# Attention stage: rounded projections with their orders, one instruction over two banks for maxima and exponentials, the last recurrence ahead of V's rows

## The chip, the core and the metric

One NeuronCore of a Trainium2 chip runs the whole program in one launch. The metric is the device time in microseconds; lower is better. The engines are PE (matmuls; PEld is its weight load), DVE (VectorE), ACT (ScalarE), POOL (GpSimd) and SP (queues DMAs). Each works through its own instructions in the order in which they are written and waits on counting semaphores for the others.

## The reference

A token tower over x of 32 sequences of 256 tokens, width D = 192: four recurrent blocks, one attention block of 12 heads of width 16, and one quantised feed-forward block.

```python
def _block(x, g, bt, Wi, bi, cw, cb, wd, bd_, wB, bB_, wC, bC_, wo, bo):
    h = _layernorm(x, g, bt)
    uv = h @ Wi.T + bi
    u, v = (uv[..., :D], uv[..., D:])
    uc = _dwconv_causal(u, cw, cb)
    delta = jax.nn.softplus(uc @ wd.T + bd_)
    Bm = uc @ wB.T + bB_
    Cm = uc @ wC.T + bC_
    y = _selective_scan(uc, delta, Bm, Cm)
    y = y * jax.nn.sigmoid(v)
    return x + (y @ wo.T + bo)
...
x = embedding[tokens] + pos_enc[:S][None]
...
h = h + _L0_attn_ref(_layernorm(h, axis=-1), wq, bq, wk, bk, wv, bv, wo, bo)
h = h + _L0_ffn_ref(_layernorm(h, axis=-1), weight_t, bias)
```

The attention takes q (scaled by 1/4), k and v from three projections of the normalised rows, turns part of q and k by the rope angles, and computes softmax(q k^T) v and an output projection. The normalisation in front of it has no gain or bias.

## The kernel before

**Two stages.** Rows lie in `x` (SBUF) from the first gather to the end. The first stage (`steps`, 67 steps) runs 64 items, 16 for each of the four layers, an item being four tiles of 128 rows (two sequences). The second stage (`steps2`, 37 steps, m = 2 to 38) runs 32 sequences of 256 rows through attention and feed-forward. Both are software pipelines written out by hand: in a step, every engine does a different piece of the work for items of different lags. `at(k)` is the item or sequence k steps behind. Nothing sets the order but the text of each engine's `step` and `step2` and the semaphores.

**Step 2 on PE** has six groups g = 0 to 5. In each: the transposed scores of `at(4)` (`scores_t`, L759, four matmuls over 64 rows, into banks `B_ST`), the plain scores of `at(2)` (`scores`, L746, into `B_S`, for the row maxima), the transposes that turn the heads of `at(2)` (`turn_heads`, L732, `identr,parts`), and something of its own. Group 0 ends with `turn_x1` (L704 and L706, `ident,xn`) and has the last of the value products (`values`, L775, also in groups 2 and 4); group 1 begins with `turn_max` (L787) and ends with `project_qk` for the first 128 rows (L711, L712); group 2 has `turn_back` (L816) and ends with `project_qk` for the other 128 rows; group 3 ends with `project_v` (L718, L721); group 4 has `turn_o` (L704, L706), group 5 begins with `project_o` (L718, L721 with `w_out`) and ends with `feed_forward`.

**The projections** of Q, K and V take full f32 operands: `h1_t`, the turned rows, as the stationary operand, in two parts of 128 and 64 rows of the contraction, and `w_qkv` as the moving one. The program has one matmul for each part; the trace shows each full-f32 matmul as two instructions. Transposes and everything declared `F32R` are one instruction each.

**Their input.** `norm_rows` (DVE, L1395) writes (x - mean) * rstd of two tiles to `xn1`; `turn_x1` turns it into `B_H1`; `save_h1` (ACT, `turned`, L1061 and L1062) copies it to `h1_t`. `inverse_deviation2` (POOL, L466 to L478, seven small instructions) gives `rstd2` for it and for the second normalisation `xn2` of `at(6)`.

**The chains around the scores.** `maxima` (DVE, L1406) reduces each of the two score banks with an instruction of its own. `exps` (ACT, L1071) does the same with exponentials of the two `B_ST` banks. `scores` of a group waits for `maxima` of the group before and for `save_heads` (ACT, L1081 and L1082) of its own; `scores_t` of a group waits for `exps` of the group before. ACT's order in a group is `exps`, `save_heads`, then, in group 0, `save_o` (L1110, L1111) and `save_h1`; `save_max` (L1103) opens group 1; `high_parts` (L1092) ends groups 3 and 4. `save_qk` (DVE, L1416) takes q and k from their banks; POOL's `rotate` turns them, ACT's `high_parts` rounds them, POOL's `low_parts` (the end of `rotate`, L499) takes the remainder; `parts` is what `turn_heads` of the next step turns. `quantise` is DVE's three passes on `xn2` (L1456, L1459, L1464), `finish` its last one (L1473).

**The seam.** In the last step of the first stage, `step` at l = 4, k = 2, the attention of sequence 0 begins. DVE does `save_qk` twice and `save_v`; then, in `step2` at m = 2 (`early`), the `recurrence` of the last item (L1319 to L1341). PE's `rows` of that item (L676 to L686) needs its `hc_l` (L1341).

## Time and profile before

| | us |
|---|---|
| median of 3 runs | 1655.63 (1651.02 to 1657.86) |
| the profiled execution | 1659.81 |
| its span from the first instruction to the last | 1657.9 |
| PE busy in the span | 1555.3 (94%) |
| DVE busy | 1365.5 (82%) |
| ACT busy | 1238.9 (75%) |
| POOL busy | 747.5 (45%) |

The span is what the trace covers; 1.9 us of the profiled execution lie outside it. Busy time counts a matmul from its start to the end of its last write, so PE can show as busy while the next matmul could not yet start; the distance from one start to the next is the measure for what a matmul costs.

### The profile page before, as it was taken

How to read it: one execution, taken by the hardware profiler on the slowest of the kernel's cores; microseconds unless marked ns; L12 is line 12 of the kernel's file. 1: busy time of each engine (PE TensorE's matmuls, PEld its weight loads, DVE VectorE, ACT ScalarE, POOL GpSimd, SP SyncE). 2: the span in 40 equal slices, each digit the busy share in tenths (PEclk: the TensorE clock that was granted, in tenths of full speed). 3: DMA queues.
4: the chain of work that ended last, by engine and by line, in shares of the span. 5: the costliest groups of instructions: out<-in, count | busy, mean ns of one | idle time of the engine just before them, and what ended most of it. 6: DMA issues, size and time to landing. Idle time of an engine off the chain costs nothing.

```text
span 1657.9 us, 36360 instructions
## 1 busy us (share of the span) xinstructions
PE 1555.3 (94%) x11137; PEld 1229.3 (74%) x11137; DVE 1365.5 (82%) x3414; ACT 1238.9 (75%) x2875; POOL 747.5 (45%) x1354
## 2 busy tenths in 40 slices
PE   3699999999999999999999988999999999999985
PEld 2578788878888888888888875666666666666653
DVE  4699999889999899999999875678888878888864
ACT  2587788688888778888888844677777777777763
POOL 6656633223333233333333244555565555555542
PEclk9799999999999999999999995999999999999997
DMA  7121100000000000000000000000000000000000
GB/s 165 31 59 28 23 8 1 1 33 0 0 1 1 1 1 0 0 1 1 1 0 0 1 1 1 2 7 11 11 10 15 10 10 10 10 10 10 15 12 25
DMA packets 16397, 21.98 MB, mean 13 GB/s; under 512 B 2928, under 2 KB 13808, under 8 KB 16304
## 3 DMA queue, kind: packets, MB, share of 16 engines
q1 hardware_dynamic: 13232, 14.54, 2.7%
q0 software_dynamic: 3072, 6.30, 2.4%
q8 instruction: 47, 0.77, 0.2%
q14 instruction: 46, 0.38, 0.1%
HBM read 14.14 MB, written 6.29 MB: 12 GB/s over the span
## 4 chain that ended last, share of the span: by engine, by line
PE 62%; ACT 14%; DVE 12%; issue 9%; POOL 1%; DMA 1%; DVEq 1%; ACTq 0%; POOLq 0%
PE bank L595 9%; PE bank L586 7%; PE bank L775 5%; PE bank L732 4%; PE bank L746 4%; PE bank L718 4%; PE bank L759 4%; PE bank L711 3%; PE bank L721 3%; PE bank L712 3%; PE bank L676 3%; ACT xs L1028 2%; DVE x L1360 2%; ACT ht L1018 2%; PE bank L606 2%
## 5 line engine op out<-in xcount | busy, mean ns | idle before, releaser
L1071 ACT ACTIVATE probs<-bank 128x512 f32<-128x512 f32 x384 | 207.1, 591 | 133.8 <-PE bank L759 131.0
L1406 DVE TENSOR_REDUCE mx<-bank 128x2 f32<-128x512 f32 x384 | 246.1, 682 | 26.6 <-PE bank L746 25.0
L441 POOL TENSOR_TENSOR x<-x,bo_row 128x768 f32<-128x768 f32 (+1 forms) x64 | 118.9, 1858 | 188.0 <-DVE ucr_r L1305 188.0
L586 PE MATMUL bank<-ht,w_uv 128*128 128x512 f32 x576 | 171.0, 407 | 16.5 <-ACT sv_l L1051 11.5
L759 PE MATMUL bank<-q_t,k_t 64*128 64x256 f32 x768 | 157.2, 353 | 8.7 <-ACT probs L1071 5.5
L417 POOL TENSOR_TENSOR lnt<-mv,const 128x4 f32<-128x4 f32 x64 | 20.5, 321 | 311.9 <-DVE mv L1270 311.8
L746 PE MATMUL bank<-k_t,q_t 64*128 64x256 f32 x768 | 141.2, 325 | 6.2 <-ACT k_t L1082 3.1
L1296 DVE SCALAR_TENSOR_TENSOR uc_h<-u_h,vec,uc_h 128x512 f32<-128x512 f32 x192 | 143.9, 750 | 2.9 <-ACT uc_h L989 2.9
L586 PEld LDWEIGHTS bank<-ht,w_uv 128*128 128x128 f32 x576 | 111.2, 196 | 46.3 <-issue 16.6
L1279 DVE SCALAR_TENSOR_TENSOR xs<-x,rstd,xs 128x192 fp32r<-128x192 f32 x256 | 90.0, 413 | 59.4 <-ACT xs L1028 59.4
L759 PEld LDWEIGHTS bank<-q_t,k_t 64*128 64x128 f32 x768 | 103.0, 188 | 39.7 <-issue 21.3
L499 POOL TENSOR_TENSOR parts<-qk_rows,parts 128x192 fp32r<-128x192 f32 x128 | 77.8, 628 | 99.9 <-ACT parts L1092 99.8
L586 PE MATMUL bank<-ht,w_uv_rest 128*128 128x512 f32 x384 | 122.0, 400 | 0.0
L968 ACT ACTIVATE u_l<-bank,vec 64x256 f32<-64x256 f32 x128 | 60.0, 469 | 78.1 <-PE bank L586 77.3
L985 ACT ACTIVATE uc_l<-bank,vec 64x256 f32<-64x256 f32 x128 | 71.9, 561 | 60.9 <-DVE inp_l L1322 59.9
L595 PE MATMUL bank<-ucr_h,w_z 128*128 128x512 f32 x256 | 107.5, 420 | 5.6 <-ACT ht L1018 5.4
L746 PEld LDWEIGHTS bank<-k_t,q_t 64*128 64x128 f32 x768 | 99.1, 194 | 16.0 <-ACT k_t L1082 9.1
L732 PE MATMUL bank<-identr,parts 128*128 128x128 f32 x768 | 105.9, 263 | 2.2 <-issue 2.1
L1081 ACT ACTIVATE q_t<-bank 128x256 fp32r<-128x256 f32 x192 | 73.5, 383 | 45.0 <-PE bank L732 44.9
L775 PE MATMUL bank<-probs,v_aug 128*32 128x256 f32 x1536 | 104.5, 390 | 0.2 <-issue 0.2
L1018 ACT ACTIVATE ht<-bank 128x512 fp32r<-128x512 f32 x192 | 100.8, 598 | 4.8 <-PE bank L647 3.3
L647 PE MATMUL bank<-identr,xs 128*128 128x128 f32 x768 | 76.2, 247 | 29.1 <-DVE xs L1279 18.3
(178 smaller groups left out, 4668.9 us busy)
## 6 DMA issues: line engine op xcount, KB each, us to landing
out_dram<-y_out SPq DMA_DIRECT2D x32, 192.0 KB, 2.0
raw_z<-w_z_dram SPq DMA_DIRECT2D x4, 704.0 KB, 5.3
raw_uv<-w_uv_dram SPq DMA_DIRECT2D x4, 576.0 KB, 3.9
emb<-embedding_dram,idx POOLq DMA_INDIRECT x64, 3.6
q_t<-mx_t SPq DMA_DIRECT2D x64, 6.0 KB
w_o<-w_o_dram SPq DMA_DIRECT2D x1, 768.0 KB, 5.4
bo_row<-bout_dram SPq DMA_DIRECT2D x4, 96.0 KB, 6.6
w_qkv<-w_qkv_dram SPq DMA_DIRECT2D x1, 288.0 KB, 7.1
```

What stands on the lines that cost most here:

```text
L441: nc.gpsimd.tensor_tensor(rows, rows, bo_row[:, l, :][:, None, :].broadcast_to([P, CT, D]), ALU.add).then_inc(x_biased, 1)
L586: last = nc.tensor.matmul(out[:], w, r[:], start=(k == 0), stop=(k == len(passes) - 1))
L595: last = nc.tensor.matmul(out[:], w, r[:, b, :], start=(k == 0), stop=(k == len(passes) - 1))
L732: last = nc.tensor.transpose(B_HEADS[g][:, (2 * o + t) * P:(2 * o + t + 1) * P].bitcast(F32R), parts[:, s, t, o, 2 * g:2 * g + 2, :].rearr ...
L746: last = nc.tensor.matmul(B_S[j][:, t * S:(t + 1) * S], q_t[q, s, g, t * P:(t + 1) * P], k_t[q, s, g, :], start=True, stop=True)
L759: last = nc.tensor.matmul(B_ST[j][:, t * S:(t + 1) * S], k_t[q, s, g, t * P:(t + 1) * P], q_t[q, s, g, :], start=True, stop=True)
L775: last = nc.tensor.matmul(bank[32 * h:32 * h + 32, c:c + S], v_aug[:, s, t, 4 * p + h, :], probs[:, (s + p) % 2, h // 2, (2 * (h % 2) + t) ...
L1018: last = act.activation(ht[g][:], B_T[g][:], ACT.Identity)
L1071: last = act.activation(probs[:, (s + g // 2) % 2, g % 2, 2 * j * S:2 * (j + 1) * S], B_ST[j][:], ACT.Exp, scale=float(DH) ** -0.5)
L1279: last = nc.vector.scalar_tensor_tensor(out=xs[:, k, D:2 * D], in0=x[:, tile_of(c, k)], scalar=rstd[:, s, k:k + 1], in1=xs[:, k, 0:D].bitc ...
L1296: nc.vector.scalar_tensor_tensor(out=uc, in0=uk, scalar=v(l, part, V_W0 + k), in1=uc, op0=ALU.mult, op1=ALU.add).then_inc(taps, 1)
L1406: last = nc.vector.tensor_reduce(mx[:, s, :, j * H // 2 + g], B_S[j][:].rearrange("p (t k) -> p t k", t=2), AX, ALU.max)
```

## The change

- PSUM is declared as four pairs of banks instead of eight banks. The two score banks are neighbours now, and so are the two banks of transposed scores. `maxima` and `exps` become one instruction over both banks.
- The Q, K and V projections take F32R operands in five passes over 128 contraction rows each: the rounded rows and the rest of the rows, packed in three groups of 128, against rounded weights, and two more passes against the rest of the weights. The weights are centred beforehand (their column means subtracted), so that the rows need no mean subtracted.
- `norm_rows` for `xn1` becomes `round_rows2` on POOL (x * rstd, rounded, both tiles in one instruction) and `rest_of_rows2` on DVE (x * rstd less the rounded part). `turn_x1` is six F32R transposes in two halves (four at the end of group 0 into `B_H1`, two in group 1 after `turn_max` into the other half of `B_MT`'s bank); `save_x1` copies them in two instructions, the second at the head of group 1.
- The weights are loaded in layer 0 (SP, after the last gather is placed) and prepared in layer 3: means in steps 3 and 4 (PE), centring in steps 4 and 5 (DVE), rounding in step 14 (ACT), the rest in step 15 (DVE).
- POOL's order in a step is `inverse_deviation2`, `rotate` of the first 128 rows, `round_rows2`, V's rows, `rotate` of the others, `low_parts`. The third pass of `quantise` moves from the end of a step to the next one, behind `norm_variances`. On ACT in group 4, the copies of the turned output (`B_OTT`) go ahead of `exps`.
- At the seam, the last `recurrence` is split and stands between and behind the two `save_qk`, ahead of `save_v`.

```diff
-            return ctx.enter_context(nc.psum_tensor(name, [P, 512], F32))
+            return ctx.enter_context(nc.psum_tensor(name, [P, 2, 512], F32))
...
-        w_qkv = sb("w_qkv", [P, 2, 3 * D])
+        w_qkv = sb("w_qkv", [P, 3, 3 * D], F32R)
+        w_qkv_rest = sb("w_qkv_rest", [P, 2, 3 * D], F32R)
...
-        xn1 = sb("xn1", [P, 2, 2, D])
-        h1_t = sb("h1_t", [P, 2 * S])
+        xs1 = sb("xs1", [P, 2, 2, 2 * D], F32R)
+        h1_t = sb("h1_t", [P, 2, 3, P], F32R)
...
-        (B_UH, B_VH, B_UVL, B_ZH, B_ZCL, B_BH, B_BL, B_CH) = [ps(f"bank{i}") for i in range(8)]
+        banks = [ps(f"banks{i}") for i in range(4)]
+        (B_UH, B_ZH, B_BH, B_BL, B_VH, B_UVL, B_ZCL, B_CH) = [banks[i // 2][:, i % 2, :] for i in range(8)]
...
+        QKV_SPREAD, QKV_MEANS, QKV_CENTRE, QKV_ROUND, QKV_SPLIT = 2, (3, 4), (4, 5), 14, 15
+        QKV_COLS = ((0, 2 * D), (2 * D, 3 * D))
...
+        B_SS, B_SST = banks[1][:], banks[0][:]
...
+                if l == 1:
+                    sp.wait_ge(x_loaded, NCH)
+                    sp.dma_start(raw_qkv, w_qkv_d).then_inc(s_w2, 16)
...
+            def rounded_there(m, it):
+
+                if it is not None:
+                    wait(pool, rstd2_ready, m + 1)
+                    wait(pool, t1_done, 2 * (it[0] - 1))
+
+            def round_rows2(it):
+                if it is None:
+                    return
+                n, s = it
+                nc.gpsimd.tensor_tensor(xs1[:, s, :, 0:D], x[:, bass.ds(n * 2 * D, 2 * D)].rearrange("p (k d) -> p k d", d=D),
+                                        rstd2[:, 0:2][:, :, None].broadcast_to([P, 2, D]), ALU.mult
+                                        ).then_inc(xs1_rounded, 1)
...
+                inverse_deviation2(at(None))
+                rounded_there(at(None), at(0))
+                if at(1) is not None:
+                    rotate(at(1), 0)
+                round_rows2(at(0))
...
-                inverse_deviation2(at(None))
                 it = at(1)
                 if it is not None:
-                    rotate(it)
+                    n, s = it
+                    rotate(it, 1)
+                    for t in range(2):
+
+                        wait(pool, hi_ready, 2 * n + t + 1)
+                        if t == 1 and at(0) is not None:
+
+                            wait(pool, xn1_ready, at(0)[0] + 1)
+                        low_parts(s, t)
...
+            def qkv_mean(part):
+
+                lo, hi = QKV_COLS[part]
+                pe.wait_ge(s_w2, W2_ALL)
+                pe.wait_ge(mean_spread, 1)
+                nc.tensor.matmul(B_VH[:, 0:hi - lo], gain_rows[:, 0, :], raw_qkv[:, 0, lo:hi], start=True, stop=False)
+                nc.tensor.matmul(B_VH[:, 0:hi - lo], gain_rows[0:LO, 1, :], raw_qkv[0:LO, 1, lo:hi], start=False,
+                                 stop=True).then_inc(qkv_means, 1)
...
-                rows_turned(xn1[:, s], B_H1, ident[:]).then_inc(t1_done, 1)
+                for k, (t_, g_) in enumerate(X1_PARTS[4:] if second else X1_PARTS[:4]):
+                    dst = B_H2[:, S + k * P:S + (k + 1) * P] if second else B_H1[:, k * P:(k + 1) * P]
+                    last = nc.tensor.transpose(dst.bitcast(F32R), xs1[:, s, t_, g_ * P:(g_ + 1) * P], identr[:])
+                last.then_inc(t1_done, 1)
+
+            def qkv_product(t_, cols, dst):
+                passes = ((0, w_qkv[:, 0, cols]), (1, w_qkv[:, 1, cols]), (2, w_qkv[:, 2, cols]),
+                          (0, w_qkv_rest[:, 0, cols]), (1, w_qkv_rest[:, 1, cols]))
+                for k, (g_, w) in enumerate(passes):
+                    last = nc.tensor.matmul(dst, h1_t[:, t_, g_, :], w, start=(k == 0), stop=(k == len(passes) - 1))
+                return last
...
-                wait(pe, h1_ready, n + 1)
-                rows_times(h1_t, t, w_qkv, slice(0, 2 * D), B_QK[t][:, 0:2 * D]).then_inc(qk_done, 1)
+                wait(pe, h1_ready, 2 * n + 2)
+                qkv_product(t, slice(0, 2 * D), B_QK[t][:, 0:2 * D]).then_inc(qk_done, 1)
...
-                both_rows_times(h1_t, w_qkv, slice(2 * D, 3 * D), B_V).then_inc(v_done, 1)
+                for t in range(2):
+                    last = qkv_product(t, slice(2 * D, 3 * D), B_V[:, t * D:(t + 1) * D])
+                last.then_inc(v_done, 1)
...
+                if l == L - 1 and k in QKV_CENTRE:
+                    pe.wait_ge(qkv_centred, 3 * (QKV_CENTRE.index(k) + 1))
...
-                for j in range(2):
-                    last = act.activation(probs[:, (s + g // 2) % 2, g % 2, 2 * j * S:2 * (j + 1) * S], B_ST[j][:], ACT.Exp,
-                                          scale=float(DH) ** -0.5)
-                last.then_inc(exp_done, 1)
+                act.activation(probs[:, (s + g // 2) % 2, g % 2, :].rearrange("p (j k) -> p j k", j=2), B_SST, ACT.Exp,
+                               scale=float(DH) ** -0.5).then_inc(exp_done, 1)
...
+                        if at(1) is not None:
+                            save_x1(at(1)[0], True)
                         save_max(at(3))
-                    exps(at(4), g)
                     if g == 4 and at(5) is not None:
                         turned(B_OTT, or_t, ott_done, at(5)[0], ott_saved)
+                    exps(at(4), g)
                     save_heads(at(2), g)
...
+            def centre_qkv(part):
+
+                lo, hi = QKV_COLS[part]
+                dve.wait_ge(qkv_means, part + 1)
+                for p in range(3):
+                    nc.vector.tensor_tensor(raw_qkv[:, p, lo:hi], raw_qkv[:, p, lo:hi], B_VH[:, 0:hi - lo],
+                                            ALU.subtract).then_inc(qkv_centred, 1)
+
+            def split_qkv():
+                dve.wait_ge(qkv_rounded, 3)
+                for p in range(2):
+                    nc.vector.tensor_tensor(w_qkv_rest[:, p, :], raw_qkv[:, p, :], w_qkv[:, p, :].bitcast(F32),
+                                            ALU.subtract).then_inc(qkv_split, 1)
...
+            def rest_of_rows2(m, it):
+                if it is None:
+                    return
+                n, s = it
+                wait(dve, xs1_rounded, n + 1)
+                for k in range(2):
+                    last = nc.vector.scalar_tensor_tensor(out=xs1[:, s, k, D:2 * D], in0=x[:, rows_of(n, k)],
+                                                          scalar=rstd2[:, k:k + 1], in1=xs1[:, s, k, 0:D].bitcast(F32),
+                                                          op0=ALU.mult, op1=ALU.subtract)
+                last.then_inc(xn1_ready, 1)
...
-                for j in range(2):
-                    last = nc.vector.tensor_reduce(mx[:, s, :, j * H // 2 + g], B_S[j][:].rearrange("p (t k) -> p t k", t=2),
-                                                   AX, ALU.max)
-                last.then_inc(max_done, 1)
+                nc.vector.tensor_reduce(mx[:, s].rearrange("p t (j h) -> p j t h", j=2)[:, :, :, g],
+                                        B_SS.rearrange("p j (t k) -> p j t k", t=2), AX, ALU.max).then_inc(max_done, 1)
...
                     save_qk(seq(0), 0)
+                    recurrence_high(item(ITEMS - 1))
                     save_qk(seq(0), 1)
+                    recurrence_rest(item(ITEMS - 1))
                     save_v(seq(0))
...
+                if l == L - 1 and k == QKV_SPREAD:
+                    dve.wait_ge(means_done, L)
+                    nc.vector.memset(gain_rows[:], 1.0 / D).then_inc(mean_spread, 1)
+                if l == L - 1 and k == QKV_SPLIT:
+                    split_qkv()
...
-                    recurrence(item(ITEMS - 1))
...
                     norm_variances(first, second)
+                quantise(at(7), 2)
                 save_qk(at(1), 0)
...
-                if first is not None:
-                    wait(dve, t1_done, first[0] - 1)
-                norm_rows(m, first, 0, xn1[:, at(0)[1]] if first is not None else None, xn1_ready)
+                rest_of_rows2(m, first)
...
-                quantise(second, 2)
```

PE, the last steps written out before the loop of the second stage, from the last values of group 0 to `turn_back` of group 2. Before:

```order
L775 MATMUL bank<-probs,v_aug 32x256 x8
L704 MATMUL bank<-ident,xn 128x128 x2
L706 MATMUL bank<-ident,xn 64x128 x2
L787 MATMUL bank<-ident,mx 12x128 x2
L759 MATMUL bank<-q_t,k_t 128x256 x4
L746 MATMUL bank<-k_t,q_t 128x256 x4
L732 MATMUL bank<-identr,parts 128x128 x4
L711 MATMUL bank<-w_qkv,h_t 128x384
L712 MATMUL bank<-w_qkv,h_t 128x384
L759 MATMUL bank<-q_t,k_t 128x256 x4
L746 MATMUL bank<-k_t,q_t 128x256 x4
L816 MATMUL bank<-ident,o_t 128x128 x3
```

The same place after the change:

```order
L829 MATMUL banks<-probs,v_aug 32x256 x8
L854 MATMUL banks<-identr,xs 128x128 x4
L841 MATMUL banks<-ident,mx 12x128 x2
L854 MATMUL banks<-identr,xs 128x128 x2
L813 MATMUL banks<-q_t,k_t 128x256 x4
L800 MATMUL banks<-k_t,q_t 128x256 x4
L786 MATMUL banks<-identr,parts 128x128 x4
L861 MATMUL banks<-w_qkv,h_t 128x384 x3
L861 MATMUL banks<-w_qkv_rest,h_t 128x384 x2
L813 MATMUL banks<-q_t,k_t 128x256 x4
L800 MATMUL banks<-k_t,q_t 128x256 x4
L885 MATMUL banks<-ident,o_t 128x128 x3
```

Two of the six transposes of the rows now stand behind `turn_max`, and a projection is five matmuls in a row.

DVE, the same steps, from the end of one to the middle of the next. Before:

```order
L1406 TENSOR_REDUCE mx<-bank 128x2 x2
L1464 TENSOR_SCALAR xq<-xn 128x384
L1473 SCALAR_TENSOR_TENSOR y_out<-bank,x 128x384
L1406 TENSOR_REDUCE mx<-bank 128x2 x2
L1379 BN_STATS st<-x 128x6 x4
L1406 TENSOR_REDUCE mx<-bank 128x2 x2
L1386 BN_AGGR mv<-st 128x2 x4
L1416 TENSOR_TENSOR qk_rows<-bank,b_qkv 128x384
```

After the change:

```order
L1521 TENSOR_REDUCE mx<-banks 128x2x2
L1587 SCALAR_TENSOR_TENSOR y_out<-banks,x 128x384
L1521 TENSOR_REDUCE mx<-banks 128x2x2
L1484 BN_STATS st<-x 128x6 x4
L1521 TENSOR_REDUCE mx<-banks 128x2x2
L1491 BN_AGGR mv<-st 128x2 x4
L1578 TENSOR_SCALAR xq<-xn 128x384
L1530 TENSOR_TENSOR qk_rows<-banks,b_qkv 128x384
```

The write of `xq` has moved past `y_out`, two maxima and both statistics instructions.

DVE at the seam, from the last rows of `x` of the second-last item on. Before:

```order
L1416 TENSOR_TENSOR qk_rows<-bank,b_qkv 128x384 x2
L1425 COPY v_rows<-bank 128x384
L1319 SCALAR_TENSOR_TENSOR inp_h<-bank,vec,uc_h 128x512
L1322 SCALAR_TENSOR_TENSOR inp_l<-bank,vec,uc_l 128x256
L1328 SCALAR_TENSOR_TENSOR hs_h<-dc_h,inp_h 128x256 x2
L1332 SCALAR_TENSOR_TENSOR hs_l<-dc_l,inp_l 128x256
L1337 SCALAR_TENSOR_TENSOR hc_h<-bank,vec,hs_h 128x512
L1341 TENSOR_TENSOR hc_l<-cb_l,hs_l 128x256
```

After the change:

```order
L1530 TENSOR_TENSOR qk_rows<-banks,b_qkv 128x384
L1419 SCALAR_TENSOR_TENSOR inp_h<-banks,vec,uc_h 128x512
L1422 SCALAR_TENSOR_TENSOR inp_l<-banks,vec,uc_l 128x256
L1428 SCALAR_TENSOR_TENSOR hs_h<-dc_h,inp_h 128x256 x2
L1530 TENSOR_TENSOR qk_rows<-banks,b_qkv 128x384
L1437 SCALAR_TENSOR_TENSOR hs_l<-dc_l,inp_l 128x256
L1442 SCALAR_TENSOR_TENSOR hc_h<-banks,vec,hs_h 128x512
L1446 TENSOR_TENSOR hc_l<-cb_l,hs_l 128x256
L1539 COPY v_rows<-banks 128x384
```

The recurrence's first half fills the time between the two `save_qk`, and the copy of V's rows comes last.

## Rows read from the trace of the kernel before

**Rows 1.** Windows: engine busy us in each stretch, granted PE clock, DMA share, GB/s.

```profile
1072.50:1552.50 480.00, 472.15 (x4197) 320.50 (x4193) 388.78 (x900) 360.32 (x1023) 278.67 (x550) 1.00 0.03 10
```

**Rows 2.** Timeline, PE, one step: start, length in us, instruction, [idle before].

```profile
1250.97 0.91 PE L711 MATMUL bank<-w_qkv,h_t 128*128 128x384 f32 x2
...
1254.39 0.92 PE L718 MATMUL bank<-w_qkv,h_t 128*128 128x192 f32 x4
...
1256.55 0.44 PE L704 MATMUL bank<-ident,o_rows 128*128 128x128 f32 x2
...
1264.16 0.44 PE L704 MATMUL bank<-ident,xn 128*128 128x128 f32 x2
...
1264.93 0.38 PE L787 MATMUL bank<-ident,mx 128*12 128x128 f32 x2
1265.24 0.50 PE L759 MATMUL bank<-q_t,k_t 64*128 64x256 f32 x4
...
1265.91 0.54 PE L732 MATMUL bank<-identr,parts 128*128 128x128 f32 x4
1266.28 0.88 PE L711 MATMUL bank<-w_qkv,h_t 128*128 128x384 f32 x2
...
1267.53 0.38 PE L746 MATMUL bank<-k_t,q_t 64*128 64x256 f32 x1
...
1268.41 0.55 PE L816 MATMUL bank<-ident,o_t 128*128 128x128 f32 x3
...
1270.21 0.91 PE L711 MATMUL bank<-w_qkv,h_t 128*128 128x384 f32 x2
```

**Rows 3.** Timeline, PE, F32R passes of a recurrent layer, 512 and 256 columns.

```profile
405.29 0.39 PE L595 MATMUL bank<-ucr_h,w_z_rest 128*128 128x512 f32 x1
405.52 0.40 PE L595 MATMUL bank<-ucr_l,w_z_rest 128*128 128x512 f32 x1
...
406.10 0.28 PE L606 MATMUL bank<-ucr_h,w_z_rest 128*128 128x256 f32 x1
406.22 0.28 PE L606 MATMUL bank<-ucr_l,w_z_rest 128*128 128x256 f32 x1
```

**Rows 4.** Lines, PEld over the span: busy us, mean ns, idle before.

```profile
L606 PEld LDWEIGHTS bank<-ucr_r,w_z 128*128 128x128 f32 x128 | 24.4, 191 | 0.0
```

**Rows 5.** Timeline, ACT, groups 0 to 1 of the step of rows 2.

```profile
1265.84 1.05 ACT L1071 ACTIVATE probs<-bank 128x512 f32<-128x512 f32 x2
...
1267.06 0.36 ACT L1082 ACTIVATE k_t<-bank 128x256 fp32r<-128x256 f32 x1
```

**Rows 6.** Timeline, DVE and POOL, end of the step of rows 2.

```profile
1259.11 0.36 DVE L1459 TENSOR_SCALAR xn<-xn 128x384 f32<-128x384 f32 x1
...
1261.90 1.00 POOL L456 TENSOR_TENSOR x<-x,b_ffn 128x384 f32 x1
1262.02 1.10 DVE L1464 TENSOR_SCALAR xq<-xn 128x384 bf16<-128x384 f32 x1
...
1263.51 1.28 DVE L1406 TENSOR_REDUCE mx<-bank 128x2 f32<-128x512 f32 x2
```

**Rows 7.** Timeline, PE, the seam, with its idle time and what ended it.

```profile
987.44 1.05 PE L680 MATMUL bank<-ones,hc_h 128*128 128x1 f32 x8 [3.60 <-DVE hc_l L1341]
```

**Rows 8.** Windows about the seam, columns as in rows 1.

```profile
980.00:990.00 10.00, 6.40 (x43) 5.45 (x42) 6.49 (x11) 1.66 (x6) 5.96 (x9) 0.93 0.00 1
...
1040.00:1045.00 5.00, 4.86 (x31) 2.10 (x29) 1.51 (x4) 1.29 (x4) 1.30 (x3) 0.68 0.00 0
```

**Rows 9.** Timeline, PE and DVE, means and centring ahead of a recurrent layer.

```profile
546.30 0.91 PE L571 MATMUL bank<-raw_uv,gain_rows 128*128 128x384 f32 x2 [0.82 <-ACT sv_h L1054]
...
549.96 1.67 DVE L1204 SCALAR_TENSOR_TENSOR raw_uv<-raw_uv,gain,bank 128x384 f32<-128x384 f32 x3 [2.32 <-PE bank L577]
```

**Rows 10.** Timeline, PE, one projection of Q and K soon after rows 7.

```profile
993.35 1.61 PE L711 MATMUL bank<-w_qkv,h_t 128*128 128x384 f32 x2
...
997.23 0.72 PE L732 MATMUL bank<-identr,parts 128*128 128x128 f32 x4 [0.27 <-issue]
```

132 lines of the change are left out of this document (82 added, 50 removed).

## The prediction, made before the changed kernel was run

> **What bounds the kernel now.** I read the busy shares by stretch first, then PE's timeline of one step of the second stage, then the other engines' timelines of that step, and last the seam between the stages. In 480 us of the second stage PE is busy for 472, DVE for 389, ACT for 360 and POOL for 279, at full clock [rows 1]. A step takes 19.24 us: from the second Q/K projection (L711) at 1250.97 to the same at 1270.21 [rows 2]. The 480 us are 25 such steps. PE works through a fixed list in order, and nearly every start follows the one before at the pace of its work, so the step is PE's list plus a few short waits. Two waits show. `turn_max` (L787) starts at 1264.93, though the four transposes ahead of it began at 1264.16 and four of them need about 0.5 us: it waited for DVE's last maxima, which ran from 1263.51 to 1264.79 [rows 2, 6]. And the score matmul at 1267.53 starts 0.11 us after ACT's copy of k (1267.06 + 0.36) ends [rows 2, 5]; there the Q/K projection fills most of the wait, since its 64-row half and the scores run side by side.
>
> The change takes work off PE in each step with a projection. So the questions are how much, and what is late next.
>
> **Q and K.** From the first L711 (1266.28) to `turn_back` (L816, 1268.41) pass 2.13 us, eight score matmuls among them. The same eight alone, in group 1, take 1265.24 to 1265.91, 0.67 us [rows 2]. So one projection of 128 rows costs 1.46 us, the two of a step 2.9. Afterwards each is five F32R passes of 384 columns. An F32R pass of 512 columns takes 0.23 us from start to start and one of 256 takes 0.12 [rows 3]; between them lies 0.175. Five are 0.87 us, ten are 1.75. Gain 1.2 us.
>
> **V.** 1254.39 to 1256.55 is 2.16 us, less 0.67 is 1.49 [rows 2]. Afterwards it is ten passes of 192 columns. No row shows that width. The bounds are a four-transpose group of 128 columns (1265.91 to 1266.28, 0.09 each, which a matmul of more columns cannot well undercut) and 0.12 for 256 columns [rows 2, 3]: 0.9 to 1.2 us. I take 0.95, nearer the lower end, because the time per column holds from 512 down to 256. Gain 0.54.
>
> **The turned rows.** Four full-f32 transposes (some 0.5 us) become six F32R ones at 0.09, so 0.54: nothing gained, and the second pair costs perhaps 0.1 for the change of form.
>
> **The moved pass of `quantise`.** It takes 1.10 us at 1262.02, beside a POOL addition that runs from 1261.90 to 1262.90, where a pass over as many elements takes 0.36 when nothing is beside it [rows 6]. It stands ahead of the maxima that `turn_max` waits for. Moved behind the statistics, where POOL is waiting for those very statistics, it should take about 0.4. The 0.25 us wait ahead of `turn_max` goes. The Trainium skill (SBUF — State Buffer, "Who interferes with whom") says that a DVE instruction in a two-port mode, or with two SBUF inputs against a GpSimd instruction that reads SBUF, blocks for the whole of the other. The two rows agree. The same rule speaks against another part of this change: `rest_of_rows2` has two SBUF inputs where `norm_rows` had one. By it, two such instructions of 0.4 us may be held for up to the 1.0 us of a POOL addition.
>
> **One instruction over two banks.** Two exponentials take 1.05 us from the first start to the last end, two maxima 1.28 [rows 5, 6]. They overlap already, so one instruction over both should end about 0.05 us sooner. The next PE work waited for the second of each pair anyhow. No operation over two banks is in the trace; I bound it between 0.1 us better and 0.2 worse per instruction, twelve a step, and only ACT's and DVE's spare time pays. On PE I take nothing.
>
> **POOL's new work.** `round_rows2` handles 384 elements, as L456 does in 1.00 us [rows 6]. POOL goes from 58% of the step to about 69% of a shorter one. It runs before V's rows and the second `rotate`, and `rest_of_rows2` waits for it, as does all behind that on DVE (V's rows, xn2, the maxima of group 3). Counting from the statistics (7 small instructions, 2.7 us; the first `rotate`, 1.9; this, 1.0) it is done some 0.7 us before DVE asks for it. `low_parts` would end about 1 us before `turn_heads` wants it. I cost it at nothing, with these margins as the cover.
>
> **What is late next.** PE's list gets shorter by 1.2 + 0.54 + 0.25 - 0.1 = 1.9 us. But the wait on ACT in group 1 is no longer covered. ACT must now do the second `save_x1` (about 0.26 more) ahead of `save_max` and the exponentials of group 1, which began at 1265.84 and ended at 1266.89; the heads' copies follow and ended at 1267.42 [rows 5]. PE will be through with its projection at the time at which it used to be halfway, stands before `scores_t`, then before the scores that need k. Laid out from the values' end on, these scores come 0.4 us later than PE alone would reach them. Elsewhere I found the chains of DVE (`turn_back`, `normalise`, maxima of group 2) and ACT just in time. So the step gains 1.5 us: 17.7. 27 steps (m = 5 to 31) run at this length: **-40.5 us**.
>
> **The seam.** PE stands for 3.60 us until `hc_l` of the last recurrence is there [rows 7]. The recurrence now starts between the two `save_qk`, so this wait closes; a Q/K and a V projection ahead of it are 1.1 us shorter as well. The heads need POOL's `low_parts` then, and I count 4 us. In the window with this wait the granted clock falls to half, 1.2 GHz: 0.93 in 980 to 990, and back only in 1040 to 1045 (0.68) [rows 8], that is about 988.6 to 1043.2. In it one Q/K projection with its scores takes 3.88 us (993.35 to 997.23) against 2.13 at full clock [rows 2, 10]. If the clock stays low as long as before, F32R saves about 1.1 us on each of three projections in each of three steps: 10 us, so 14 with the wait. If it never falls, the ramp is about 27 us shorter in all. The wait that came before the fall is gone, but the ramp's own waits on ACT stay. I take **-20**, between the two.
>
> **The new preparation in layer 3.** PE's means of a layer start after 0.82 us of waiting, and L571 and L572 take 0.85 each; DVE's three centring instructions over 384 columns take 1.67, and PE needs them [rows 9]. For Q and K: 0.8 + 1.7 + 1.9 = 4.4 us, with nothing beside it, since PE's wait stands ahead of everything in the next step. For V, half the columns: 0.8 + 0.85 + 1.2 = 2.9. Rounding on ACT (three over 576 columns, 1.8 us) and the rest on DVE (1.5 us) lie in single steps with about that much idle time. Together **+7** (4 to 10).
>
> **The tail.** Steps m = 32 and 33 have a projection and its wait less: **-2.5**. The start has two DMAs fewer on SP; nothing waits there.
>
> **Sum.** Against the profiled execution's 1659.8 (span 1657.9 and 1.9 around it): -40.5 - 20 - 2.5 + 7 = -56, so 1604. The median of the three runs is 4.2 below the profiled one; by it 1600.
>
> **Rivals.** (a) *Another engine keeps the step long.* If ACT's chain in group 1, DVE behind `rest_of_rows2`, or POOL's `low_parts` is later than I laid out, the step is 18.3 to 18.8: 27 x 0.6 to 1.1 = 16 to 30 us less gain, 1616 to 1630, with a low clock at the seam up to 1640. For it: the margins are 0.1 to 1 us. Against it: DVE and ACT have 19% and 25% idle. (b) *No wait remains and the clock holds at the seam*: 17.3 a step and -27 at the seam, 1575 to 1585. (c) *Slower.* If every full-height pass had to wait for its own weight load, 0.19 us [rows 4], with nothing beside it, a 384-column pass would cost 0.365 and a 192-column one 0.285: 3.65 + 2.85 = 6.5 us against 4.4 now. The step would be about 21 us and the kernel about 1700. It decides from a pass of 0.22 us on average, 4.4 / 20. Against it stand 256-column passes at 0.12 apart with loads of that very length [rows 3, 4]. The skill (TensorE: Matmul & The Clock Gate, "The mechanism") states such a rule: a weight load overlaps running matmuls only where the row group differs, although it also grants a background weight buffer. The rows speak for the buffer. (d) *It does little*: PE's gain is eaten by a DVE or ACT instruction over two banks that costs much more than two; 1650 to 1660.
>
> **Chances.** Forecast (1585 to 1616): 0.64. (a) 0.16; (b) 0.12; (c) 0.04; (d) 0.04. A measurement tells about 0.5% from no change, 8 us. So faster 0.92, same 0.04, slower 0.04. The range takes in the forecast and most of (a) and (b): 1578 to 1630.
>
> **What would show it.** Steps 17.7 us apart by the turned rows' transposes; Q/K passes 0.175 apart, V passes 0.095; the moved `quantise` pass at about 0.4 us and no wait ahead of `turn_max`; a wait of PE on ACT in group 1; no idle PE before the last `hc` products; and the length of the half-clock stretch. The forecast falls if the V passes come at over 0.12 us, if an instruction over two banks takes over 1.2 us on ACT, or if PE waits for DVE or POOL by more than 0.5 us a step.

## The result and the profile after

The changed kernel takes **1625.8 us** (median of four runs, 1624.7 to 1627.3) beside 1656.7 us for the kernel before (four runs, 1651.0 to 1660.5). The ratio is 0.983, with a 95% interval of 0.981 to 0.985. It is 1.7% faster, clear of the spread of the runs, and inside the range of 1578 to 1630, but the gain is 31 us where 56 were forecast. A second set of six runs gave 1627.7 us and 0.982 (0.979 to 0.985).

Where the 33.8 us between the two profiled executions lie, cut at the same work in both traces. The prediction's 27 steps (m = 5 to 31) are split over three of these stretches: m = 5 lies in the seam, m = 31 in the rest, and 25 between.

| stretch | before | after | difference | forecast |
|---|---|---|---|---|
| start, up to the turned rows of the 48th item | 727.1 | 727.2 | 0 | 0 |
| layer 3, to the turned rows of its last item | 219.1 | 227.3 | +8.2 | +7 |
| seam, to `turn_max` of the fourth sequence | 126.8 | 110.4 | -16.4 | -20 and -1.5 for m = 5 |
| 25 steps, to `turn_max` of the 29th | 480.2 | 457.1 | -23.1 | -37.5 |
| the rest | 104.6 | 102.3 | -2.3 | -2.5 and -1.5 for m = 31 |

So layer 3 came out near its size and the seam 5 us short of it; the rest gained little over half of its 4 us, and the large term fell shortest: the step, which went from 19.2 to 18.3 us and not to 17.7. The same stretch as [rows 1], 480 us of the second stage, by the windows of the kernel after (busy us of PE, PEld, DVE, ACT and POOL, granted clock, DMA share, GB/s), with the seam's windows below it, as [rows 8]:

```profile
1050.00:1530.00 480.00, 474.70 (x4558) 348.39 (x4557) 385.25 (x780) 378.18 (x910) 316.06 (x608) 1.00 0.03 11
...
990.00:1000.00 10.00, 8.59 (x63) 7.34 (x61) 4.54 (x10) 3.31 (x10) 6.05 (x11) 0.77 0.01 2
1000.00:1010.00 10.00, 7.05 (x48) 5.64 (x47) 8.61 (x15) 4.28 (x16) 7.44 (x18) 0.84 0.00 0
1010.00:1020.00 10.00, 9.25 (x46) 7.40 (x46) 5.53 (x10) 3.48 (x11) 5.20 (x14) 0.53 0.00 1
1020.00:1030.00 10.00, 6.76 (x52) 5.36 (x50) 7.48 (x10) 7.34 (x19) 7.46 (x12) 0.81 0.01 2
1030.00:1040.00 10.00, 9.72 (x82) 7.61 (x80) 6.26 (x10) 6.68 (x16) 6.38 (x15) 0.85 0.00 1
```

PE is busy for 98.9% of the stage, where it was 98.4%: the list got shorter, and it is still PE's list that sets the step. At the seam the clock's 0.77, 0.84, 0.53, 0.81 and 0.85 mean 24 us at half clock (each tenth below 1 is 2 us of such a 10 us window), where it used to be 54.6.

One step on PE, which answers to [rows 2] (start, length, instruction):

```profile
1265.07 0.53 PE L854 MATMUL banks<-identr,xs 128*128 128x128 f32 x4
1265.44 0.38 PE L841 MATMUL banks<-ident,mx 128*12 128x128 f32 x2
...
1265.87 0.50 PE L813 MATMUL banks<-q_t,k_t 64*128 64x256 f32 x4
...
1266.62 0.54 PE L786 MATMUL banks<-identr,parts 128*128 128x128 f32 x4
1267.19 0.79 PE L861 MATMUL banks<-w_qkv,h_t 128*128 128x384 f32 x3
...
1268.98 0.55 PE L885 MATMUL banks<-ident,o_t 128*128 128x128 f32 x3
...
1270.75 0.79 PE L861 MATMUL banks<-w_qkv,h_t 128*128 128x384 f32 x3
...
1271.82 0.50 PE L813 MATMUL banks<-q_t,k_t 64*128 64x256 f32 x4
...
1273.75 0.58 PE L861 MATMUL banks<-w_qkv,h_t 128*128 128x192 f32 x3
1274.17 0.38 PE L861 MATMUL banks<-w_qkv_rest,h_t 128*128 128x192 f32 x2
1274.39 0.50 PE L861 MATMUL banks<-w_qkv,h_t 128*128 128x192 f32 x3
...
1275.04 0.50 PE L813 MATMUL banks<-q_t,k_t 64*128 64x256 f32 x4
...
1275.71 0.44 PE L764 MATMUL banks<-ident,o_rows 128*128 128x128 f32 x2
1275.99 0.38 PE L766 MATMUL banks<-ident,o_rows 128*64 128x128 f32 x2
1276.30 0.54 PE L786 MATMUL banks<-identr,parts 128*128 128x128 f32 x4
...
1283.42 0.54 PE L854 MATMUL banks<-identr,xs 128*128 128x128 f32 x4
```

Set against [rows 2], start to start, the step falls into six pieces:

| piece | before | after | gain | forecast |
|---|---|---|---|---|
| turned rows and `turn_max`, to the scores | 1.08 | 0.80 | 0.28 | 0.15 |
| first scores to `turn_back` (first Q/K) | 3.17 | 3.11 | 0.06 | 0.19 |
| `turn_back` to the second Q/K | 1.80 | 1.77 | 0.03 | 0 |
| second Q/K to V | 3.42 | 3.00 | 0.42 | 0.59 |
| V to `turn_o` | 2.16 | 1.96 | 0.20 | 0.54 |
| `turn_o` to the turned rows | 7.61 | 7.71 | -0.10 | 0 |
| whole step | 19.24 | 18.35 | 0.89 | 1.47 |

No projection gained what its passes were costed at, and a new wait stands behind `turn_o`. Those are the places that the experiments look at.

### The profile page after: what moved, and what is told of

Its sections match the earlier page's. It is cut to its first block, busy times and chain, and to the rows that moved or that the text cites. A ratio compares the mean times of both kernels' runs of the same rounds, so it can differ in the third digit from the quotient of the medians.

```text
span 1624.1 us, 36462 instructions
## 1 busy us (share of the span) xinstructions
PE 1522.8 (94%) x11337; PEld 1242.0 (76%) x11337; DVE 1345.7 (83%) x3231; ACT 1241.7 (76%) x2686; POOL 775.8 (48%) x1386
## 4 chain that ended last, share of the span: by engine, by line
PE 41%; ACT 22%; DVE 19%; issue 14%; POOL 2%; DVEq 1%; DMA 1%; ACTq 0%; POOLq 0%
PE banks L861 7%; PE banks L829 6%; PE banks L786 5%; PE banks L813 5%; DVE x L1465 5%; ACT xs L1104 4%; ACT ht L1094 4%; PE banks L800 4%; DVE xs L1376 4%; ACT dc_l L1079 2%; PE banks L637 2%; DVE hs_h L1428 2%; DVE inp_h L1419 2%; PE banks L772 2%; ACT u_h L1050 2%
## 5 line engine op out<-in xcount | busy, mean ns | idle before, releaser
L1521 DVE TENSOR_REDUCE mx<-banks 128x4 f32<-128x1024 f32 x192 | 234.1, 1219 | 44.8 <-PE banks L800 44.2
L1152 ACT ACTIVATE probs<-banks 128x1024 f32<-128x1024 f32 x192 | 195.8, 1020 | 85.3 <-PE banks L813 82.0
L637 PE MATMUL banks<-ht,w_uv 128*128 128x512 f32 x576 | 171.8, 408 | 19.5 <-ACT sv_l L1127 13.7
L637 PEld LDWEIGHTS banks<-ht,w_uv 128*128 128x128 f32 x576 | 111.3, 197 | 50.0 <-issue 18.3
L637 PE MATMUL banks<-ht,w_uv_rest 128*128 128x512 f32 x384 | 122.7, 402 | 0.0
L813 PE MATMUL banks<-q_t,k_t 64*128 64x256 f32 x768 | 108.9, 333 | 7.0 <-ACT probs L1152 5.1
L646 PE MATMUL banks<-ucr_h,w_z 128*128 128x512 f32 x256 | 107.7, 421 | 6.1 <-ACT ht L1094 5.3
L786 PE MATMUL banks<-identr,parts 128*128 128x128 f32 x768 | 104.3, 260 | 3.9 <-issue 3.0
L698 PEld LDWEIGHTS banks<-identr,xs 128*128 128x128 f32 x768 | 73.8, 142 | 39.7 <-DVE xs L1376 18.1
L829 PE MATMUL banks<-probs,v_aug 128*32 128x256 f32 x1536 | 103.6, 388 | 0.1
L646 PE MATMUL banks<-ucr_l,w_z 128*128 128x512 f32 x256 | 100.9, 394 | 0.0
```

Source lines behind the costliest of these rows:

```text
L637: last = nc.tensor.matmul(out[:], w, r[:], start=(k == 0), stop=(k == len(passes) - 1))
L646: last = nc.tensor.matmul(out[:], w, r[:, b, :], start=(k == 0), stop=(k == len(passes) - 1))
L698: last = nc.tensor.transpose(B_T[g][:, k * P:(k + 1) * P].bitcast(F32R), xs[:, k, g * P:(g + 1) * P], identr[:])
L786: last = nc.tensor.transpose(B_HEADS[g][:, (2 * o + t) * P:(2 * o + t + 1) * P].bitcast(F32R), parts[:, s, t, o, 2 * g:2 * g + 2, :].rearr ...
L813: last = nc.tensor.matmul(B_ST[j][:, t * S:(t + 1) * S], k_t[q, s, g, t * P:(t + 1) * P], q_t[q, s, g, :], start=True, stop=True)
L829: last = nc.tensor.matmul(bank[32 * h:32 * h + 32, c:c + S], v_aug[:, s, t, 4 * p + h, :], probs[:, (s + p) % 2, h // 2, (2 * (h % 2) + t) ...
```

## The experiments

The same cuts for every kernel that was run, in us. "Half clock" is the part of the seam in which the granted clock was at half.

| kernel | start | layer 3 | seam (half clock) | 25 steps | rest | span |
|---|---|---|---|---|---|---|
| before | 727.1 | 219.1 | 126.8 (54.6) | 480.2 | 104.6 | 1657.9 |
| after | 727.2 | 227.3 | 110.4 (23.9) | 457.1 | 102.3 | 1624.1 |
| after, once more | 728.3 | 227.2 | 111.9 (27.3) | 456.7 | 100.6 | 1624.7 |
| no_proj | 726.3 | 219.5 | 119.0 (44.4) | 474.3 | 103.0 | 1642.1 |
| narrow | 731.3 | 227.5 | 111.2 (41.0) | 453.2 | 101.4 | 1624.6 |
| u_seam | 730.5 | 227.6 | 116.9 (30.7) | 457.0 | 102.3 | 1634.4 |
| v_first | 727.3 | 227.3 | 113.3 (30.7) | 466.5 | 102.6 | 1636.9 |
| u_merge | 732.2 | 227.4 | 111.8 (27.3) | 460.8 | 103.0 | 1635.2 |
| u_quant | 727.0 | 227.2 | 110.3 (23.9) | 457.5 | 101.0 | 1623.0 |
| late_wait | 728.2 | 223.8 | 111.2 (27.3) | 457.1 | 103.2 | 1623.6 |
| v_mid | 727.7 | 227.5 | 109.0 (17.1) | 454.3 | 101.9 | 1620.4 |
| both (best2) | 729.6 | 223.8 | 110.2 (23.9) | 454.1 | 102.3 | 1620.0 |
| wide_v | 726.1 | 227.6 | 108.8 (17.1) | 457.5 | 102.2 | 1622.2 |

None of the edits touches the start, and yet it spreads over 6 us: the four in which it holds 51 to 55 us at half clock are at 729.6 to 732.2, the others, with 34 to 41, at 726.1 to 728.3. A difference of a few us in the whole time is therefore read from the stretch that was edited and not from the span.

**no_proj: everything but the projections.** The kernel before with the change's instructions over two banks, ACT's copies of the turned output ahead of the exponentials in group 4, the moved pass of `quantise` and the last recurrence in two halves; the projections, their rows and their weights are as before.

```diff
-                save_qk(seq(0), 1)
-                save_v(seq(0))
+                recurrence_high(item(ITEMS - 1))
+                save_qk(seq(0), 1)
+                recurrence_rest(item(ITEMS - 1))
+                save_v(seq(0))
...
+                quantise(at(7), 2)
                 save_qk(at(1), 0)
```

> The kernel before with all of the change except the projections: pairs of banks with one instruction for two maxima or two exponentials, the turned output's copies ahead of the exponentials, the moved quantise pass, the split last recurrence. The projections, their input and the weights stay as before. Theory A (the gain of a step comes from the projections, and they were priced too high: 0.96 us in place of 1.74): the step falls only by the wait ahead of turn_max, 19.2 to 19.0, and the seam loses its 3.6 us; in all 8 to 12 us below the kernel before, about 1646. The half-clock stretch at the seam stays long, over 40 us. Rival B (the joined instructions and the orders carry the step's gain, and the projections give little): step at 18.6 or less, about 1635. Rival C (the closed wait alone frees the clock): the half-clock stretch shrinks to about 24 us as in the changed kernel, and the seam's gain is 16 us, about 1636 with a step of 19.0.

Measured: 1640.0 us (1635.5 to 1643.9), ratio 0.989 (0.983 to 0.994). Layer 3 is at 219.5: the whole +8.2 belongs to the new weights. The step is 18.97, as theory A has it: 0.24 of the 0.92 us of a step come from what is not a projection, the rest from the projections and their rows. The whole gain, 15.8 us between the spans, is above theory A's 8 to 12, mainly because the seam gives 7.8 of its 16.4 us here and not 3.6. Half clock still holds for 44.4 us of the seam, so rival C, by which the closed wait alone frees the clock, falls, and so does rival B.

**narrow: shorter passes.** Left out: two of the five passes of each Q/K projection, and a third of V's columns (128 in the place of 192). What is stored is therefore not the whole product.

```diff
+                if cols.start == 0:
+                    passes = passes[:3]
...
-                    last = qkv_product(t, slice(2 * D, 3 * D), B_V[:, t * D:(t + 1) * D])
+                    last = qkv_product(t, slice(2 * D, 2 * D + P), B_V[:, t * D:t * D + P])
```

> The changed kernel with V's passes over 128 of the 192 columns (a third of V is left out) and Q's and K's projections without their two passes against the rest of the weights (three passes in place of five). It measures the price of a pass. Theory A (a pass of few columns is floored by its weight load at 0.11 us, and each group of passes has fixed edges): V's passes stay 0.11 apart though a third of their columns is gone; Q's and K's lose 2 x 2 x 0.175 = 0.7 us; the step goes from 18.3 to 17.6. Rival D (the distance goes with the columns, plus 0.03): V's passes at 0.085, the step at 17.4.

Measured: 1626.5 us in one run. That is no faster, but the 25 steps are 3.9 us shorter, and the start, with 14 us more at half clock, is 4.1 longer. A step gains 0.16 us and not the 0.7 of theory A: 18.1 and not 17.6. PE's timeline of this kernel:

```profile
1270.90 0.79 PE L863 MATMUL banks<-w_qkv,h_t 128*128 128x384 f32 x3
...
1272.25 0.50 PE L800 MATMUL banks<-k_t,q_t 64*128 64x256 f32 x4
1272.68 0.55 PE L887 MATMUL banks<-ident,o_t 128*128 128x128 f32 x3
...
1274.46 0.79 PE L863 MATMUL banks<-w_qkv,h_t 128*128 128x384 f32 x3
1275.17 0.50 PE L813 MATMUL banks<-q_t,k_t 64*128 64x256 f32 x4
...
1277.11 0.55 PE L863 MATMUL banks<-w_qkv,h_t 128*128 128x128 f32 x3
1277.50 0.39 PE L863 MATMUL banks<-w_qkv_rest,h_t 128*128 128x128 f32 x2
1277.72 0.50 PE L863 MATMUL banks<-w_qkv,h_t 128*128 128x128 f32 x3
...
1278.37 0.51 PE L813 MATMUL banks<-q_t,k_t 64*128 64x256 f32 x4
```

and ACT's of the same group:

```profile
1271.84 0.36 ACT L1164 ACTIVATE k_t<-banks 128x256 fp32r<-128x256 f32 x1
```

Four things are to be read in this kernel. *V:* the ten passes take 1.26 us (1277.11 to 1278.37) with 128 columns and 1.29 (1273.75 to 1275.04) with 192. The third of the columns that is gone was free: the two `w_qkv_rest` passes of the first tile take 0.22 us in both kernels, 0.11 each, as theory A has it; rival D's 0.085 falls. *Second Q/K:* three passes take 0.71 us (1274.46 to 1275.17), five take 1.07 (1270.75 to 1271.82), so a pass costs 0.18, as forecast; but three times 0.18 is 0.53. The other 0.18 us belong to the group, not to its passes. *First Q/K:* two passes less bring nothing. The plain scores start at 1272.25, 0.05 us after ACT's copy of k ends (1271.84 + 0.36), and `turn_back` stands 1.78 us behind the projection's start, as in the kernel after (1267.19 to 1268.98, 1.79). In this group ACT sets the time, whatever the projection costs. *V's copy:* PE's list is 0.38 us shorter, 0.35 of it from the second Q/K to V (3.00 to 2.65), and more than half of that goes into a wait behind `turn_o`. From `turn_o` to the heads behind it (L764 to L786) pass 0.41 us when nothing waits, as in the kernel before; in the kernel after it is 0.53 and 0.59 in turn, in this one 0.88 and 0.65. What comes late is DVE's copy of V's rows. The waits on PE, with the total, the number and the longest, and DVE's timeline in one such step:

```profile
PE banks L786 <- DVE v_rows L1541: 2.2, 10, 0.2
```

```profile
1187.25 1.29 DVE L1512 SCALAR_TENSOR_TENSOR xs<-x,rstd,xs 128x192 fp32r<-128x192 f32 x2
```

POOL's V addition runs there from 1186.89 to 1187.90, and the first of the two instructions of `rest_of_rows2`, 0.87 us long, ends 0.22 us behind it. So a PE that is faster ahead of this point loses more than half of its gain to a longer wait at it.

**wide_v: longer passes.** V's passes with 256 columns; 64 columns of K's product are computed once more beside V's and not used.

```diff
-                    last = qkv_product(t, slice(2 * D, 3 * D), B_V[:, t * D:(t + 1) * D])
+                    last = qkv_product(t, slice(3 * D - 2 * P, 3 * D), B_V[:, 2 * t * P:2 * (t + 1) * P])
```

> The changed kernel with V's ten passes 256 columns wide in the place of 192 (64 columns of K's product are computed once more beside V's and left in the bank; V's copy takes the other 192 of each). With 128 columns V's passes were as far apart as with 192 (0.11 us). Theory A (a pass has a least length of 0.11 us, under which its columns don't count, and from there on it goes by its columns: 0.12 for 256, as the passes of the kernel before show): the passes at 0.118 to 0.122, V's projection 1.29 to 1.37 us. Theory B (its length is a fixed part plus columns, by 0.176 for 384 and 0.111 for 192, so 0.13 for 256): 0.13 apart, 1.48 us.

Measured: 1624.1 us in one run, and in PE's timeline of this kernel:

```profile
1271.93 0.62 PE L861 MATMUL banks<-w_qkv,h_t 128*128 128x256 f32 x3
1272.39 0.40 PE L861 MATMUL banks<-w_qkv_rest,h_t 128*128 128x256 f32 x2
1272.62 0.51 PE L861 MATMUL banks<-w_qkv,h_t 128*128 128x256 f32 x3
...
1273.30 0.50 PE L813 MATMUL banks<-q_t,k_t 64*128 64x256 f32 x4
```

Two passes in 0.23 us, ten in 1.37: theory A. With 128, 192, 256 and 384 columns a pass takes 0.11, 0.11, 0.118 and 0.176 us. From 192 columns down its length no longer goes by its columns, and a group pays about 0.2 us on top at its two ends. Together this gives 0.2 + 10 x 0.11 = 1.3 for V, and 0.2 + 5 x 0.176 = 1.08 for Q and K. That V's passes have 192 columns and not 256 is worth 0.08 us in all. What sets the least distance of 0.11 us is not shown: the weight loads of these passes, 0.19 us long each, start 0.11 us apart as well, and no run has one without the other. The steps of this kernel are as long as before (25 in 457.5 us beside 457.1), though V takes 0.08 us more: the wait behind `turn_o` is that much shorter (0.43 and 0.50 us to the heads).

**v_first: V's copy ahead of the rows.** In the kernel after, `turn_heads` of group 4 (L786) starts at 1276.30, 0.31 us behind the two transposes ahead of it (L766, 1275.99), where 0.14 us would do (v_mid, below). It waits for V's bank, which DVE's copy frees. DVE's and POOL's timelines of the kernel after there:

```profile
1274.75 1.03 DVE L1510 SCALAR_TENSOR_TENSOR xs<-x,rstd,xs 128x192 fp32r<-128x192 f32 x2
1275.70 0.55 DVE L1539 COPY v_rows<-banks 128x384 f32<-128x384 f32 x1
```

```profile
1273.82 1.02 POOL L580 TENSOR_TENSOR v_aug<-v_rows,b_qkv 128x384 f32<-128x384 f32 x1
```

`rest_of_rows2` (L1510) starts at 1274.75 while POOL is still in its V addition, lasts 1.03 us, and V's copy ends at 1276.25. The edit turns the two round:

```diff
-                rest_of_rows2(m, first)
                 save_v(at(1))
+                rest_of_rows2(m, first)
```

> The changed kernel with DVE's copy of V's rows ahead of rest_of_rows2. In group 4 PE's turn_heads starts 0.05 us after that copy ends, and the two instructions of rest_of_rows2 ahead of it take 1.03 us beside POOL's work where norm_rows took 0.66. Theory E (this wait is real): the group's transposes start 0.17 us earlier, the step goes from 18.3 to 18.15, 4 to 5 us less in all, about 1621. Rival: PE's list hides it, no change within 1 us; or the later rest_of_rows2 pushes the second normalisation and the maxima of group 3, and the step gets longer.

Measured: 1638.8 us (1638.1 to 1645.9), ratio 0.991 (0.987 to 0.994), some 13 us slower than the change, and the 25 steps are 9.4 us longer (about 1.8 of it in one step, in which the clock stood at half for 3.4 us). The expectation fell, and its rival came true. PE's wait is gone, but DVE's timeline shows what came for it:

```profile
1263.03 0.56 DVE L1539 COPY v_rows<-banks 128x384 f32<-128x384 f32 x1 [0.34 <-PE banks L861]
1263.51 1.47 DVE L1510 SCALAR_TENSOR_TENSOR xs<-x,rstd,xs 128x192 fp32r<-128x192 f32 x2
1264.91 1.22 DVE L1500 TENSOR_SCALAR xn<-x,mv,rstd 128x192 f32 x2
```

DVE stands idle for 0.34 us until V is there, then the two instructions fall beside the four POOL instructions of `rotate` (1262.89 to 1264.77) and take 1.47 us in the place of 1.03. The next two, L1500, take 1.22 for 0.94. The maxima of the next group come 1.1 us later within the step than in the kernel after, PE waits for them, and every other step is 18.96 us long.

The length of these instructions follows one pattern. In the kernel after, 56 of the 64 of `rest_of_rows2` end 0.20 to 0.23 us behind the end of a POOL instruction that reads SBUF and was running beside them; the other eight take 0.41 or 0.42 us: two stand alone, two run beside a POOL memset of 1.37 us, and four start within the last 0.15 us of a POOL instruction. The longest of all, 1.15 us, is the first of these two, which starts 0.08 us into POOL's V addition:

```profile
1021.33 1.57 DVE L1510 SCALAR_TENSOR_TENSOR xs<-x,rstd,xs 128x192 fp32r<-128x192 f32 x2
```

```profile
1021.25 1.02 POOL L580 TENSOR_TENSOR v_aug<-v_rows,b_qkv 128x384 f32<-128x384 f32 x1
```

This agrees with the rule that the prediction cited from the Trainium skill (SBUF — State Buffer, "Who interferes with whom"): the DVE instruction is held until POOL's is through, for up to the whole of it, and what it costs is a matter of when it starts.

**v_mid: V's copy between the two.**

```diff
-                rest_of_rows2(m, first)
+                rest_of_rows2(m, first, (0,))
                 save_v(at(1))
+                rest_of_rows2(m, first, (1,))
```

> The changed kernel with save_v between the two instructions of rest_of_rows2. With save_v behind both, PE's turn_heads of group 5 waits 0.18 us a step for V's copy from the ninth step on, when the first of the two lasts 0.61 us beside POOL in the place of 0.41 (steps of 18.36 and 18.27 in the place of 18.10). With save_v ahead of both, that wait was gone, but both instructions fell beside POOL's products of rotate (0.80 and 0.75 us) and the maxima of group 4 came 1.1 us later: 18.31 and 18.96, slower. Theory A (only the copy's place counts): V's copy ends ahead of the heads' turn, the second instruction alone slips by 0.5 us and takes at most 0.25 more: steps of 18.1 to 18.2, 1621 to 1624. Theory B (VectorE and GpSimd share access, so that what DVE gains in one place it loses in the next): the second instruction takes 0.75, the xn2 instructions and the maxima of group 4 come 0.3 to 0.5 later, steps of 18.3 to 18.7, 1626 to 1636.

Measured: 1623.6 us (1621.2 to 1626.5), ratio 0.979 (0.976 to 0.981); the steps are 18.17 and 18.20, the 25 of them 2.8 us shorter. DVE's timeline of this kernel:

```profile
1273.25 0.59 DVE L1510 SCALAR_TENSOR_TENSOR xs<-x,rstd,xs 128x192 fp32r<-128x192 f32 x1
1273.77 0.55 DVE L1540 COPY v_rows<-banks 128x384 f32<-128x384 f32 x1
1274.24 0.58 DVE L1510 SCALAR_TENSOR_TENSOR xs<-x,rstd,xs 128x192 fp32r<-128x192 f32 x1
```

V's copy now ends at 1274.32, 10.38 us into the step (it begins with `turn_max` at 1263.94), and not 10.81 (1276.25 - 1265.44). The second instruction of the rows is at 0.58 and not at 0.75: theory A, by and large. The ratio's interval touches that of the change (0.981 to 0.985); it is the steps that tell the two apart. On PE the heads follow the two transposes after 0.14 us:

```profile
1274.49 0.38 PE L766 MATMUL banks<-ident,o_rows 128*64 128x128 f32 x2
1274.63 0.54 PE L786 MATMUL banks<-identr,parts 128*128 128x128 f32 x4
```

**u_quant and u_merge: two parts undone.** Either is the change with one part as it was before.

```diff
-                quantise(at(7), 2)
                 save_qk(at(1), 0)
...
                 maxima(at(2), 4)
+                quantise(second, 2)
```

> The changed kernel with one part undone: the second pass of quantise (xq from xn) stands again behind the maxima of group 4, beside a POOL addition. The forecast's term for the move was 0.25 us a step. Theory A (it holds): the pass takes about 1.1 us again in the place of 0.32, the step is 18.5 to 18.6 in the place of 18.3, the time 1631 to 1634. Theory B (DVE is now busy without a gap from the maxima of group 3 to the end of the step, so all of the longer pass comes on top, less the 0.3 us that DVE has there): +0.5 to +0.8 us a step, 18.8 to 19.1, 1640 to 1648. Theory C (the pass was paid for elsewhere, since in the new place it stands ahead of save_qk): no change, 1624 to 1628.

Measured: 1625.5 us (1624.8 to 1630.6), ratio 0.980 (0.978 to 0.983); the 25 steps are at 457.5 beside 457.1. No difference, theory C. DVE's timeline of u_quant:

```profile
1281.61 0.63 DVE L1578 TENSOR_SCALAR xq<-xn 128x384 bf16<-128x384 f32 x1
...
1282.63 1.21 DVE L1521 TENSOR_REDUCE mx<-banks 128x4 f32<-128x1024 f32 x1
```

Back in its old place the pass takes 0.63 us, not the 1.10 of [rows 6], and the last maxima end at 1283.84, while PE reaches `turn_max` only at 1284.11. So the wait ahead of `turn_max` is away without the move. It is away in u_merge as well, which has the move but not the joined maxima; no run of the changed kernel has neither.

```diff
-                act.activation(probs[...], B_SST, ACT.Exp, ...).then_inc(exp_done, 1)
+                for j in range(2):
+                    last = act.activation(probs[...], B_ST[j][:], ACT.Exp, ...)
+                last.then_inc(exp_done, 1)
```

(and the same for the maxima.)

> The changed kernel with one part undone: the maxima and the exponentials are again two instructions over one bank each (24 instructions a step in the place of 12). Seen so far: one maximum over two banks lasts 1219 ns on average and one exponential 1020 ns, where the pairs of before lasted 1.28 us and 1.05 us. Theory A (the pair and the one cost the same to whoever waits): the steps stay within 0.05 us of the changed kernel's 18.3, the time within 3 us of 1626. Theory B (the later end of the pair is on the path, since in the narrow kernel PE waits for a copy that stands behind an exponential on ACT, and DVE is busy without a gap from the maxima of group 3 to the end of the step): 0.03 us per pair on a path that passes some six of them, so a step of 18.4 to 18.6 and 1629 to 1634. Theory C (one instruction over two banks holds up PE, which could fill the first bank again while the second is read): the undone kernel is faster, 18.1 to 18.2 a step and 1621 to 1624.

Measured: 1633.3 us (1632.0 to 1637.0), ratio 0.984 (0.982 to 0.986), step 18.44, 25 steps 3.7 us longer: 0.15 us a step, theory B at its lower end. The ratios of the two kernels don't differ; the reading rests on the 25 steps, which in the kernels that leave the second stage as it is take 456.7 to 457.1 us. In ACT's timeline of u_merge a pair lasts 1.04 to 1.09 us, where the groups of the page after have one instruction (busy us, mean ns):

```profile
L1521 DVE TENSOR_REDUCE mx<-banks 128x4 f32<-128x1024 f32 x192 | 234.1, 1219 | 44.8 <-PE banks L800 44.2
L1152 ACT ACTIVATE probs<-banks 128x1024 f32<-128x1024 f32 x192 | 195.8, 1020 | 85.3 <-PE banks L813 82.0
```

Of the 11 us between the spans of u_merge and the kernel after, 5.0 lie in the start, which the edit doesn't touch.

**u_seam: the last recurrence whole again, behind V's copy.**

```diff
-                    recurrence_high(item(ITEMS - 1))
                     save_qk(seq(0), 1)
-                    recurrence_rest(item(ITEMS - 1))
                     save_v(seq(0))
...
                 if early:
+                    recurrence(item(ITEMS - 1))
                     dve.wait_ge(x_updated, ITEMS - 1)
```

> The changed kernel with the last recurrence whole again and behind save_v, in the first step of the second stage. Theory A: PE waits some 3.6 us again for the last hc products, 1626 becomes 1630, and since the F32R projections work the array more densely the half-clock stretches stay short in all (24 us now, under 35 then). Rival C (the long wait is what held the clock low for 54.6 us): the long stretch comes back and costs over 10 us more, 1640.

Measured: 1633.6 us (1630.9 to 1636.2), ratio 0.985 (0.980 to 0.990). The seam is 6.5 us longer, and the wait of [rows 7] is back on PE:

```profile
1000.41 1.86 PE L731 MATMUL banks<-ones,hc_h 128*128 128x1 f32 x8 [4.41 <-DVE hc_l L1446]
```

With the move there is no idle time ahead of this line. The long stretch at half clock does not come back with the wait (30.7 us, 54.6 in the kernel before): theory A, and rival C falls. Nor is it clear that the move shortens the stretch at all, since the other kernels with the change's recurrence and its whole projections have 17.1 to 30.7 us of half clock there. By no_proj, which has the move and 44.4 us, most of the shortening comes with the projections. The ratios of this kernel and of the change overlap; its seam, 116.9 us beside 108.8 to 113.3 in the others with the change, does not.

**late_wait: PE's wait in layer 3 moved.** By the waits of the kernel after between 768 and 806 us PE waits twice for DVE's centring (in total, times, longest):

```profile
PE banks L637 <- DVE emb L1318: 2.6, 2, 1.6
```

```diff
-                if l == L - 1 and k in QKV_CENTRE:
-                    pe.wait_ge(qkv_centred, 3 * (QKV_CENTRE.index(k) + 1))
...
                 wait(pe, sv_ready, n)
+                if qkv is not None:
+                    pe.wait_ge(qkv_centred, qkv)
                 uv_product(l, UV_V, B_VH).then_inc(uv_done, 1)
```

> The changed kernel with one edit: in the two steps of layer 3 in which the QKV weights are centred, PE's wait for qkv_centred stands ahead of the V product of uv and no longer ahead of the whole of uv, so that PE has the U product to do while DVE centres. In the changed kernel PE waits there 1.6 and 1.1 us, and the granted clock falls to half for 3.4 us from 780.4. The two step intervals are 19.23 and 16.34 us in the place of 13.69. Theory A (the wait is what shows): both waits vanish, the clock does not fall, the intervals come to about 17.0 and 15.2, the kernel to 1621.5 to 1624. Theory B (DVE's centring is only pushed on, and the recurrence behind it on DVE then makes PE wait in the same step): the intervals keep their sum within 0.5 us, no change.

Measured: 1625.7 us (1619.5 to 1628.5), ratio 0.979 (0.976 to 0.982). Layer 3 takes 223.8 us, 3.5 less; the two long intervals are 16.45 and 15.26 us in the place of 19.23 and 16.34, and the clock stays up there. In the same window PE waits once for DVE's centring, for 0.2 us.

Theory A for the stretch. In the span only 0.5 of the 3.5 us show, since the start was 1.0, the seam 0.8 and the rest 0.9 us longer in this execution.

**Both edits.** `v_mid` and `late_wait` together, beside the change itself on the same chip, six runs each.

> The changed kernel with two edits together: save_v between the two instructions of rest_of_rows2 (alone it made 26 steps 2.9 us shorter, 472.4 for 475.3) and PE's wait for qkv_centred moved behind the U product in layer 3 (alone it made the two long intervals 35.57 to 31.71 us). Theory A (the two lie in different stages and add up): 26 steps in 472.4 us, the intervals at 31.7, the kernel 6.5 us below the changed kernel run beside it. Theory B (what layer 3 wins is lost at the seam or in the start, as the late-wait kernel's span was only 0.5 us below the changed kernel's): 3 us below it.

> The changed kernel once more, unedited, beside the version with two edits and the kernel before on the same chip, as the measure for it. Every theory: a step of 18.3, 1624 to 1628, a ratio to the kernel before of 0.979 to 0.983.

Measured: 1620.8 us (1616.3 to 1623.5) and 0.978 (0.975 to 0.981) for the two edits, 1627.7 (1622.3 to 1629.4) and 0.982 (0.979 to 0.985) for the change. The medians are 6.8 us apart; layer 3 is 3.4 and the 25 steps are 2.6 us shorter, so the two add up. This is the fastest version of the study, though the intervals of the two ratios overlap a little.

## Why the prediction was right, and where not

**The step that failed** is the gain of a step of the second stage: 1.5 us in the forecast, 0.92 in the runs, so 23.1 us over 25 steps and not 37.5. Two of its terms were wrong. The price of the F32R passes was too low (V 0.95 us where 1.29 was measured, Q and K 0.87 where 1.07 was). And `rest_of_rows2` on DVE was costed at nothing: V's copy behind it comes late for PE by 0.12 and 0.18 us in turn, and by 0.47 and 0.24 when PE's list is shorter (narrow). So a right price of the passes alone would not have saved the forecast.

**The bound.** Right. PE's list sets the step before and after; its busy share in the stage went from 98.4% to 98.9%. But its list carries more waits for DVE and ACT than the forecast gave it.

**V, the term that was most mis-sized.** I took 0.95 us for ten passes of 192 columns, and took the time per column, which holds from 512 down to 256, to hold nearly down to there. It doesn't: a pass costs 0.11 us with 128 columns and with 192, 0.118 with 256 (narrow, wide_v), and the group's ends some 0.2. The row that I put at the lower bound, four transposes at 0.09 each, is of another kind of instruction, and I reckoned its pitch, not a group with its ends. 1.29 us against 0.95: 0.34 of the 0.58 us that the step is short of the forecast. The upper end of my own bounds, 1.2, was nearer. This is where PE stands longer, and not yet what a cheaper V would have brought: wide_v made V 0.08 us longer and the step stayed, narrow took 0.38 us off PE's list and the step fell by 0.16. With V's copy where it is, passes at the forecast price would have left the step near 18.1, by my estimate from narrow's 18.13.

**Q and K.** Pitch right (0.175 forecast, 0.176 to 0.18 measured), group wrong: 1.07 us and not 0.87, by the same 0.2 us for the ends. I took five pitches against the difference of two positions in the timeline, and that difference (1.46) did have the ends of its group in it. In the second Q/K this is the whole shortfall, 0.42 us for 0.59. In the first it changes nothing, since there ACT decides. That step of the forecast stands: `save_x1` pushes ACT's copy of the maxima and the exponentials back, as ACT's timeline after shows against [rows 5],

```profile
1265.96 0.88 ACT L1143 ACTIVATE h_t<-banks 128x512 fp32r<-128x512 f32 x2
1266.70 0.36 ACT L1183 ACTIVATE mx_t<-banks 12x256 fp32r<-12x256 f32 x1
1266.97 1.00 ACT L1152 ACTIVATE probs<-banks 128x1024 f32<-128x1024 f32 x1
```

the exponentials starting 1.53 us behind `turn_max` where it was 0.91. But I had the wait at the wrong place: PE stands ahead of the projection too, which begins at 1267.19, 0.13 us after the copy that frees its bank ends (1267.06), when the four transposes ahead of it (1266.62, 0.09 each) were through at about 1266.98. The group gains 0.06 us and not 0.19.

**What is late next.** `rest_of_rows2` was costed at nothing, with the margin of 0.7 us by which its input is ready. The input was in time. What I left out is how long it lasts, though the prediction names the collision with POOL itself: two inputs from SBUF, 1.03 us for two beside a POOL addition. V's copy is then 0.18 us late for the heads of group 4. In early steps the first of the two takes 0.41 us and not 0.61, nothing waits, and the step is 18.10 (PE's `turn_max` from start to start); from the eighth on it is some 18.27 and 18.36 in turn. v_mid takes out 0.13 us of it. That it is this order is shown by v_mid. That the length is due to POOL is read from the traces alone, but closely: the same instruction took 0.41 to 1.15 us, and wherever it took more than 0.42 it ended some 0.21 us behind a POOL instruction. No run has POOL's work taken away.

**The moved pass of `quantise`.** The pass itself did as forecast (0.32 us and not 1.10), and the wait ahead of `turn_max` went, 0.28 us for 0.25. But the move was not needed for it: u_quant has the old place and neither the wait nor a longer step. Moving an instruction off a chain is worth what the chain is late by, and in the changed kernel DVE's maxima are early there anyhow. In no_proj, where PE's list is the old one, the same 0.28 us are gone; whether by the move or by the joined maxima was not run apart.

**Instructions over two banks.** Costed at nothing on PE; the runs gave 0.15 us a step (u_merge). If they are worth the same in no_proj, they are more than half of its 0.24 us.

**The seam.** -16.4 for -21.5 with the step m = 5 in both. That step gained 0.8 us, so the seam itself 15.6, near the lower end of the 14 to 27. The wait for the recurrence went (0 for 3.60 us), and u_seam puts the move at 6.5 us, with a spread of 3 us in the seam of kernels that don't touch it. The clock still falls, in three stretches of 6.8, 10.2 and 6.8 us. PE still waits there for ACT's copies of k, for DVE's maxima and for POOL's parts; which of these waits the clock would need gone, no run shows.

**Layer 3.** +8.2 for +7, as built up from waits and instructions; 3.5 of it were PE's position in the queue and not work.

**The rivals.** The step came out where rival (a) has it, at 18.3, and in part for its reason. By position in PE's list, of 0.58 us 0.51 are the price of the passes on PE, 0.18 the wait for V's copy and 0.13 more of ACT's wait than forecast, less 0.24 gained elsewhere. But "DVE behind `rest_of_rows2`", which rival (a) names, would have taken most of those 0.51 back had the passes been cheaper, as narrow shows. Rival (c) is out, with 0.11 us for a pass whose weight load takes 0.19, as in [rows 4]. The rule of the Trainium skill beside it (TensorE: Matmul & The Clock Gate, "The mechanism"), that a load overlaps only another row group's matmuls, does not describe these passes; the background weight buffer that the same section grants would. That the time lies in the range is no credit to the sum: the range was drawn wide enough for rival (a).

## What to carry to other kernels

Price a group of passes by groups: the measured distance from the work ahead to the work behind, ends included, and never so many pitches against a difference of two positions. Where a width is below every width in the trace, take the least pitch that is there for the same kind of instruction, not the time per column. And for an instruction that gets a second SBUF input, look at what POOL does in that stretch: where V's copy stood among two such instructions decided between 18.2, 18.3 and 18.6 us a step. Before you make one engine's list shorter, ask which wait grows in its place: of 0.38 us taken off PE in narrow, 0.16 reached the step.

## What the runs showed of the hardware

- An F32R matmul over 128 rows with a 128-column stationary operand is 0.11 us apart from the next with 128 or 192 moving columns, 0.118 with 256, 0.176 with 384 and 0.23 with 512 [rows 3]; a group costs some 0.2 us more than its pitches.
- One ACT instruction over two PSUM banks (1024 elements) lasts 1.02 us, where two over one each take 1.04 to 1.09; one DVE maximum over both 1.22 us, where the two took 1.28 [rows 6].
- A DVE instruction with two SBUF inputs of 192 elements took 0.41 us alone or beside a POOL memset, and up to 1.15 us beside POOL instructions that read SBUF; the held ones end 0.20 to 0.23 us behind the POOL instruction (56 of 64 in the kernel after). The `xq` pass of [rows 6], 1.10 us, ends 0.22 us behind POOL's addition in the same way.
- The same start of the program spreads over 6 us from kernel to kernel, with 34 to 55 us of half clock in it.
